# Tile b of a batch is multiplied in fp32 by weight matrices of its own, and norm and results take a new order

## What is computed

```
def _gn(v, G=32, eps=1e-05): ...      # group norm over 12 channels and all pixels
x = x + _L0_conv_ref(_gn(x), L0_conv_offset)
x = x + _L1_conv_ref(_gn(x))
```

## Time and profile before

| | |
|---|---|
| time, median of 3 runs | 290.21 us (289.92 to 291.0) |
| the profiled execution: time, span | 289.43 us, 287.6 us |
| TensorE busy | 177.8 us (62%) |
| VectorE busy | 178.9 us (62%) |
| ScalarE busy | 117.4 us (41%) |
| GpSimd busy | 72.4 us (25%) |
| DMA | 70.65 MB, mean 246 GB/s |
| start; cycles 0, 1, 2; tail | 83.3; 58.6, 60.3, 52.3; 33.1 us |

### The profile page before, as it was taken

How to read it: one execution, slowest core, us unless ns; L and a number is a source line. 1 busy time by engine, 2 the same in 40 slices (tenths; PEclk the granted TensorE clock), 3 DMA queues, 4 the chain that set the end, 5 groups by cost and what they waited for, 6 DMA issues and landing times.

```text
span 287.6 us, 3917 instructions
## 1 busy us (share of the span) xinstructions
PE 177.8 (62%) x1228; PEld 89.7 (31%) x1228; DVE 178.9 (62%) x411; ACT 117.4 (41%) x179; POOL 72.4 (25%) x101
## 2 busy tenths in 40 slices
PE   1300158306529776586597981957779839899962
PEld 1200046203204524242245351412345424233420
DVE  2779745921757585745976638448966476666642
ACT  0295088013937595098038780692231001311000
POOL 0197001328600000581200004742000036720000
PEclk9999999955969999599869997799799977999998
DMA  6999999915555176399899983896874325855544
GB/s 212 400 416 407 239 289 408 411 63 162 154 172 223 75 215 263 132 312 351 279 258 320 377 293 149 267 359 234 214 274 172 147 93 170 291 217 219 219 194 170
DMA packets 23626, 70.65 MB, mean 246 GB/s; under 512 B 5952, under 2 KB 6976, under 8 KB 23024
## 3 DMA queue, kind: packets, MB, share of 16 engines
q1 hardware_dynamic: 18480, 60.90, 60.4%
q0 software_dynamic: 5120, 9.45, 10.5%
HBM read 60.89 MB, written 29.88 MB: 316 GB/s over the span
## 4 chain that ended last, share of the span: by engine, by line
PE 39%; DVE 35%; ACT 10%; issue 8%; DMA 4%; POOL 1%; DVEq 0%; SPq 0%; POOLq 0%; ACTq 0%
PE ps L825 12%; DVE ring L1272 10%; PE ps L815 8%; PE ps L730 7%; PE ps L808 6%; DVE halves L1049 5%; ACT junk L565 4%; DVE unit_half L1140 4%; DVE plain L1137 4%; ACT junk L568 4%; PE ps L711 4%; DMA ring<-x_rows,index 2%; DVE flip L1109 2%; DMA x_rows<-plain 2%; DVE parts L1265 1%
## 5 line engine op out<-in xcount | busy, mean ns | idle before, releaser
L1272 DVE SCALAR_TENSOR_TENSOR ring<-ps,out_bias,ring 128x1024 f32<-128x1024 f32 x48 | 61.5, 1282 | 36.7 <-PE ps L825 20.3
L825 PE MATMUL ps<-ring,w_c 128*128 128x512 f32 x128 | 61.0, 615 | 5.7 <-DVE ring L1272 5.6
L815 PE MATMUL ps<-parts,had_sb 128*128 128x512 f16 x128 | 41.0, 463 | 13.8 <-DVE ring L1272 9.7
L618 ACT ACTIVATE parts<-ring,scale 128x1024 f16<-128x1024 f32 x16 | 18.0, 1143 | 62.7 <-PE ps L815 50.0
L808 PE MATMUL ps<-ring,w_a 128*128 128x512 f32 x64 | 32.0, 624 | 12.8 <-DMA ring<-x_rows,index 8.5
L565 ACT ACTIVATE junk<-ring 128x1024 f32<-128x1024 f32 x32 | 36.6, 1144 | 4.0 <-DMA ring<-x_pad 2.0
L481 POOL DMA_DIRECT2D x_rows<-plain x8 | 5.0, 620 | 128.7 <-DVE plain L1137 128.7
L568 ACT ACTIVATE junk<-ring 128x1024 f32<-128x1024 f32 x32 | 36.8, 1149 | 1.0
L825 PEld LDWEIGHTS ps<-ring,w_c 128*128 128x128 f32 x128 | 23.8, 197 | 35.2 <-issue 21.7
L1265 DVE SCALAR_TENSOR_TENSOR parts<-ring,scale,parts 128x1024 f16<-128x1024 f32 x16 | 20.6, 1288 | 18.9 <-ACT parts L618 18.9
L491 POOL DMA_INDIRECT ring<-x_rows,index x24 | 24.4, 1019 | 18.6 <-issue 18.6
(11 more groups left out here) (151 smaller groups left out, 168.6 us busy)
## 6 DMA issues: line engine op xcount, KB each, us to landing
ring<-x_pad SPq DMA_DIRECT2D x16, 1536.0 KB, 12.2
out<-ring SPq DMA_DIRECT2D x48, 512.0 KB, 3.4
shifted<-x_pad SPq DMA_DIRECT2D x32, 128.0 KB, 5.0
plain<-x_pad SPq DMA_DIRECT2D x32, 128.0 KB, 3.8
x_rows<-plain POOLq DMA_DIRECT2D x8, 512.0 KB, 4.8
shifted<-x_pad SPq DMA_DIRECT2D x16, 32.0 KB, 4.4
plain<-x_pad SPq DMA_DIRECT2D x16, 32.0 KB, 3.0
x_rows<-plain POOLq DMA_DIRECT2D x16, 32.0 KB, 1.7
```

The costliest lines, as they stand in the source:

```text
L815: last = pe.matmul(ps[n % 2][:, h, :], had_sb[:, 128 * sign:128 * (sign + 1)], parts[:, n % 2, part, s, 512 * h:512 * (h + 1)], start=Fals ...
L825: last = pe.matmul(ps[n % 2][:, h, :], w_c[:, n % 4, twice, :], ring[:, 2, place_of(n), 512 * h:512 * (h + 1)], start=False, stop=True, sk ...
L1272: dve.scalar_tensor_tensor(ring[:, t, place_of(n), :], pixels_of(ps[n % 2]), out_bias[:, q % 2, t, b:b + 1], ring[:, t, place_of(n), :], A ...
```

## The change

Tile b is treated as tile c was: `tile(n, s, twice)` multiplies it in fp32 from the ring with `w_bc` (-H and 2H times the scale of b). `high`, `low` and the fp16 tile `parts` are gone; in `parts`' memory stands `result_b`, two homes of one tile into which the results of b go, since the ring's tile b is still needed by `add_b` after `result(n, 1)`. They are stored from there with semaphores `b_out` of their own. The statistics of quarter 1 are divided anew (VectorE has b of batches 4 and 5 too), and its first sums now run before the first results. The norm steps in the cycles are spread anew among products and results; a batch of a new quarter starts its products only behind all of the old one. SPq fetches shifted pixels earlier.

```diff
 def dve_tiles(i):
     if i < 2 * QUARTER:
-        return ((0, 1), (0,))[i // QUARTER]
+        return (0, 1) if i < QUARTER + 2 else (0,)
...
# SyncE
+                if t == 1:
+                    sp.dma_start(out_v[n][:, t, :], result_b[:, n % 2, :]).then_inc(b_out[n % 2], 16)
...
-            fetch(0)
+            fetch(0, 1)
+            fetch(0, 0)
...
+            fetch(1, 1, (0, 1))
             more_blocks(0)
             rows_back(0)
-            fetch(1)
+            fetch(1, 1, (2,))
+            fetch(1, 0)
             for n in range(BATCH):
-                store(n, 1)
-                store(n, 0)
                 if n >= 1 and n - 1 + RING < BATCH:
                     load(n - 1 + RING)
-                store(n, 2)
+                for t in ORDER:
+                    store(n, t)
...
+                if j == 2 and w + 2 < QUARTERS:
+                    rows_back(w + 1)
+                    fetch(w + 2, 1)
                 if j == 3 and w + 2 < QUARTERS:
-                    rows_back(w + 1)
-                    fetch(w + 2)
+                    fetch(w + 2, 0)
...
# GpSimd, weights(n): five instructions for three
-                pool.tensor_scalar(w_c[:, n % 4, 0, :], ...)
-                pool.tensor_scalar(w_c[:, n % 4, 1, :], ...)
+                for s, sign in ((0, -1.0), (1, 1.0)):
+                    pool.tensor_scalar(w_bc[:, n % 4, s, 0, :], ...)
+                    pool.tensor_scalar(w_bc[:, n % 4, s, 1, :], ...)
...
# ScalarE
-            for i in range(QUARTER, QUARTER + 2):
+            for i in range(QUARTER, 2 * QUARTER):
                 for t in act_tiles(i):
                     take_stats(i, t)
             root_second(0)
             weights(0)
-            weights_c(0)
-            for n in range(2):
-                high(n, 0)
-            for i in range(QUARTER + 2, 2 * QUARTER):
-                for t in act_tiles(i):
-                    take_stats(i, t)
+            weights_bc(0)
+            root_first(1)
...
# TensorE
-            def product(n, s, sign, stop):
-                for part in range(2):
-                    pe.wait_ge((high_done, low_done)[part][s], n + 1)
-                    for h in range(2):
-                        last = pe.matmul(ps[n % 2][:, h, :], had_sb[...], parts[...], ...)
+            def tile(n, s, twice):
+                for h in range(2):
+                    last = pe.matmul(ps[n % 2][:, h, :], w_bc[:, n % 4, s, twice, :], ring[:, 1 + s, place_of(n), ...], ...)
...
             sum_second(0)
+            sum_means(1)
             product_a(0)
+            sum_about(1)
             sum_bias(0)
...
# VectorE, result(n, t)
+                if t == 1:
+                    if n >= 2:
+                        dve.wait_ge(b_out[n % 2], 16 * (n // 2))
+                    home = result_b[:, n % 2, :]
...
# VectorE, before the cycles
             second_scale(0)
-            low(0, 0)
+            stats_at[6] = take_stats(6)
+            stats_at[7] = take_stats(7)
+            means(1)
+            spread_means(1)
+            unit_moments(1)
             bias_at[0] = second_bias(0)
-            low(1, 0)
...
+            unit_scales(1)
```

More of the change, by code:

```diff
@@ L398, in rows @@
                     return tile[32 * s:32 * s + 32, u, :], x_slot(q, at[PER_UNIT * u + s][which])
[L400 to L405, removed]
-                for u in range(UNITS):
-                    if q:
+                for u in units:
+                    if which == 1:
+                        if q:
+                            sp.wait_ge(flipped, UNITS * (q - 1) + u + 1)
+                    elif q:
                         sp.wait_ge(x1_out[u], left(u, q - 1))
@@ L410, in fetch @@
                     for s in range(PER_UNIT):
-                        home, source = rows(plain, u, s, 0)
-                        sp.dma_start(home, source).then_inc(plain_in[u], 16)
+                        home, source = rows((plain, shifted)[which], u, s, which)
+                        sp.dma_start(home, source).then_inc((plain_in, shifted_in)[which][u], 16)
             def rows_back(q):
@@ L675, in _ @@
-                if j == 3 and units:
-                    high(n + 1, 0)
-                    high(n + 2, 0)
-                    if stats_next:
-                        take_stats(ahead + 3, 2)
+                    for u in range(UNITS):
+                        centre(g + u)
+                if stats_next:
+                    take_stats(ahead, 0)
+                    take_stats(ahead, 1)
+                if stats_next:
+                    take_stats(ahead, 2)
+                    for t in range(CT):
+                        take_stats(ahead + 1, t)
@@ L682, in _ @@
+                if units:
+                    more_blocks(w + 1)
+                    root_second(w + 1)
+                    weights(n + QUARTER)
+                    weights_bc(n + QUARTER)
+                if stats_next:
+                    take_stats(ahead + 2, 0)
+                    take_stats(ahead + 2, 1)
+                if stats_next:
+                    take_stats(ahead + 2, 2)
+                    take_stats(ahead + 3, 2)
         @block.tensor
@@ new lines, in _ @@
+            for w in range(QUARTERS):
+                n, g = QUARTER * w, UNITS * (w + 1)
+                units = w + 1 < QUARTERS
+                add_b(n)
+                product_b(n + 1)
+                if units and w:
+                    sum_means(w + 1)
+                add_c(n)
+                if units and w:
+                    sum_about(w + 1)
+                product_c(n + 1)
+                product_a(n + 2)
+                if units:
+                    transposes(g)
+                add_b(n + 1)
+                product_b(n + 2)
+                if units:
+                    transposes(g + 1)
+                    convolve(g)
+                add_c(n + 1)
+                product_c(n + 2)
+                if units:
+                    transposes(g + 2)
+                    convolve(g + 1)
+                product_a(n + 3)
+                add_b(n + 2)
+                product_b(n + 3)
+                if units:
+                    convolve(g + 2)
+                add_c(n + 2)
+                product_c(n + 3)
+                if units:
+                    more_blocks(w + 1)
+                    sum_second(w + 1)
+                add_b(n + 3)
+                if units:
+                    sum_bias(w + 1)
+                add_c(n + 3)
+                if units:
+                    product_a(n + 4)
+                    product_b(n + 4)
+                    product_c(n + 4)
+                    product_a(n + 5)
```

294 lines of the change are left out of this document (99 added, 195 removed).

## The result

The changed kernel takes 277.59 us (median of 4 runs, 276.44 to 278.98) against 290.16: a ratio of 0.956 (0.952 to 0.961). Faster as forecast and inside the range of 261 to 280, but 8 us above the 269.6 predicted and outside the 266 to 273 that were given one half. Its profiled execution took 277.31 us, span 275.5; against the 268.8 that the sum gave for it, 8.5 us are missing.

| | start | cycle 0 | cycle 1 | cycle 2 | tail | span |
|---|---|---|---|---|---|---|
| before | 83.3 | 58.6 | 60.3 | 52.3 | 33.1 | 287.6 |
| predicted | 76.2 | 50.3 | 52.3 | 51.3 | 36.9 | 267.0 |
| after | 78.4 | 50.7 | 60.4 | 49.0 | 37.0 | 275.5 |

What follows compares the result with a forecast made beforehand. Bound by a chain back and forth between TensorE and VectorE, no engine full. Start -7.1, cycles -17.3 and tail +3.8 make -20.6 against the profiled 289.4: 268.8, with 0.8 for the median 269.6 us; range 261 to 280.

Steps and rivals of the forecast that it cites:

- VectorE's wait for ScalarE: Start: VectorE stands before `means(1)` until 81.9 us for quarter 1's statistics; moving them brings the first result at 76.2, not 83.3.
- The term of 0.5 us for SPq's fetches: Start: eight shifted tiles fetched before the gather cost 0.5 us, between 0 and 3.7.
- The term of 3.4: Start: TensorE's products b and c after `product_a(0)` take 3.4 us, at full clock by then.
- The term of 1.8: Each cycle: half clock behind the wait at `sum_second`; at full clock the cycle would be 1.8 us shorter.
- the two clock cases: Cycles: half clock behind the pause, as in the forecast of 269.6 us, or clock stays up, 264.2 us, chance 0.20.
- I take 1 us of waiting, in cycle 1 alone, where a load stands in front: Cycle 1: `result(5, 1)` waits 1 us for `store(3, 1)` to empty its home; bounds 0 and 6.
- the pause of 3.5 us at `sum_second`: Each cycle: TensorE waits 3.5 us with only `sum_second` in it, then runs at half clock.
- quiet is the nearer case: Cycles: the gather lands in 4.6 us as in a quiet stretch, not 10.3 as in a full one.
- Transfers become the bound: Rival, start and cycles: late gathers, a late home of b and slower fetches give 281.1 us, half of it 275; chance 0.22.
- The slower rival: Cycles 1 and 2: results of b wait 12 us in each for their homes, 292.6 us; chance 0.04.
- about 4.5 us lower: Cycles: by the skill's sentence, most of the 5.4 us for half clock over three cycles would be struck.
- by that alone the term would be 0: Start: if engines take turns between queues, GpSimd's writes don't wait for SPq's backlog, so the fetches cost 0, not 0.5 us.

Runs made afterwards that it cites:

- e9: The changed kernel with each batch's three stores issued before its load instead of the load first: 269.84 us, ratio 0.932.
- e2: The changed kernel with the load's old place, stores of b and a ahead of it and the store of c behind: 276.89 us, ratio 0.948.
- e1: The changed kernel with three homes for the results of b instead of two, ScalarE's unread output in fp16: 275.76 us, ratio 0.951.
- e10: The changed kernel with loads of batches 10 to 15 bringing one of three tiles (output not the reference's): 269.4 us, ratio 0.924.
- e15: The kernel before with the load behind all three stores of a batch: 289.25 us, ratio 0.998.
- e14: e9 with the shifted pixels of quarter 1 fetched only behind the first gather: 268.29 us, ratio 0.924.
- e4: The changed kernel with dummy products on TensorE, 16 before `product_a(0)` and 12 behind each `sum_second`: 275.9 us, ratio 0.953.

## Why the prediction was right and wrong

- **Start, -7.1 forecast, -4.9 measured.** That VectorE's wait for ScalarE goes was right. Two sizes failed. The term of 0.5 us for SPq's fetches was taken near its lower end and is about 1.6 (1.7 in this execution, of which 0.8 shows, since the writes were issued 0.8 earlier than before). And "b and c, by then at full clock" did not hold in this execution. It holds in others: of five profiles of the same program up to here two show 12.0 and 12.9 us from the gather's issue to the first result (e9, e2) and three some 15 (after, e1, e10). The term of 3.4 should have been 3.4 to 5.5.
- **Cycle 0, 50.3 forecast, 50.7 measured; the tail, 36.9 and 37.0.** Right by their own working (the tail's second sum is 33.9 by its terms, not 33.8): dense TensorE, a pause, half clock behind it, 8.6 us a batch in the tail (`result(12, 1)` 238.49, `result(13, 1)` 247.07).
- **Cycle 2, 51.3 forecast, 49.0 measured.** In this execution the clock stayed up behind the pause. Mean granted clock 1.00, and both rows behind it at 1.98. The term of 1.8 wasn't due. Other executions with the same pause did fall (e9 50.5, e10 51.2), so the two clock cases are not rivals: they alternate, within one execution.
- **Cycle 1, 52.3 forecast, 60.4 measured.** The step that failed is "I take 1 us of waiting, in cycle 1 alone, where a load stands in front", with bounds of 0 and 6. Place, cause and bounds were right and the choice was not. I took the store's median landing, 3.4 us, for a store directly behind a load and a fetch. It took 8.5: 4.3 us more than in the sum. Behind it the sum had nothing, though it had taken half clock behind the pause of 3.5 us at `sum_second`: here half clock came behind a pause of 4.18 us and cost 3.0. The third part is "quiet is the nearer case" for the gather: 9.2 us instead of 4.6 and 1.5 us of TensorE's waits. Together 8.8 for the 8.1 missing; the pause behind `sum_second`, 2.8 for 3.5, gives 0.7 back.
- **What I had not seen at all** is the chain. I priced one store behind one load, and not that the next load waits for that store. e9 shows it, and e15 that its cost was new. The diff showed one cause, the load moved to the head of the batch; e2 shows that the shorter cycles are another.
- **The rivals.** "Transfers become the bound", at 275 for the half of it and 281.1 for the whole, is what happened, and 277.6 lies between; it had 0.22. Its parts were 1.1 a cycle for the gather, 5 for the home and 3.2 at the start, over the sum; measured were 1.5 in cycle 1 alone, 4.3, and 1.1 (1.6 for 0.5). That the total fell between the two is in part luck: the half clock behind the home wait, 3.0, was in neither. The slower rival stayed far off: home waits never passed 6.0 us in any profile.
- **Two terms set beside the Trainium skill.** The Trainium skill (TensorE: Matmul & The Clock Gate, What's actually happening) says that for modeling the ramp penalty is under 1% of a typical kernel's span. Cycle 0 with and without dummies differs by 1.2 us, and the behind-home and start drops cost 3.0 and about 2: some 2% here, in rows at half clock. Nor did "about 4.5 us lower" follow from that sentence, for 1% of the 267 us predicted is 2.7, which leaves room for half of the 5.4. The Trainium skill (DMA: Bandwidth & Descriptors, Queues, rings and completion order) says that the engines take turns between queues packet by packet, and I wrote that by that alone the term would be 0. The writes landed in 6.2 us with the fetches queued (e9) and in 3.6 without (e14). Taking turns with a full queue may well be slower than having the engines alone (no run shows it directly), so this need not contradict the sentence; what I drew from it was wrong.

## What to carry to other kernels

When a change shortens a cycle, work out anew what each queue does in it: loads ahead of stores that the next load waits for cost nothing in the kernel before, with cycles of 53 to 60 us (e15), and 6.6 us in cycle 1 of the changed one, whose other cycles take 49 to 51 (e9). In a queue put what others wait for first (the stores), the big and patient transfer last, and look at what a queue's blocking wait shields, here the gather, before moving it. Price a transfer by what stands ahead of it in its queue, not by its median.

## What the runs showed that was not expected

- Taking half clock away gave the cycles nothing as long as transfers were late (e4: 1.2 us won in cycle 0, 1.2 lost in cycle 1); nor is a stall worth its length, for e1 removed one of 5.3 us and kept 2.4.
- The same instructions fall to half clock or not from one execution to the next. After the same pause of 2.8 us the pass behind it took 3.63 us in cycle 1 and 1.98 in cycle 2 of the same run.
- Dummies have a size: 32 records before the first product took 6.22 us, because they themselves ran mostly at half clock, and delayed what they were to speed up; 12 took 2.91, and the start was 3.2 us shorter, 0.3 of it the gather's.
- A stage can have two ends at one instant. In the kernel before with fp32 b the first result was released by TensorE at half clock and by VectorE's statistics within 0.1 us of each other, so a profile of one execution hid what moving the statistics is worth.
